# Mixing a convolution's spectra in two halves of the sequences, the second inside attention's first slots

## The chip, the cores and the metric

One core of a Trainium2 chip (trn2). The metric is the device time of one launch in microseconds, the median of several executions. The program is written by hand, engine by engine: each engine has one list of instructions, and semaphores are all that orders one engine against another.

## What is computed

16 sequences of 256 tokens with 256 channels pass through three stages: a spectral convolution, causal attention, and a mixture of 8 experts of which each token uses 2. Only the first two stages matter here.

```
x_ft = rfft(groupnorm(x))[..., :16]                 # 16 modes of each of 16 channels, 16 times, 16 sequences
out  = einsum('btix,iox->btox', x_ft * w_temb, w)   # "mixing": input channels i to output channels o
x    = x + irfft(out / norm)
t    = tokens(x)
t    = t + softmax(q k^T / 16, causal) v W_o        # q, k, v from layernorm(t)
t    = t + sum over top 2 of 8 experts of c_e * gelu(n W_fc[e]) W_proj[e],  n = layernorm(t)
```

## The kernel before

**Convolution.** TensorE makes the spectra z of all sequences (`spectra`), VectorE multiplies them with the time weights into `zr` and `zi`, both with sequence and time as columns (16 x 16 = 256). Mixing is then 4 output groups `og`, each a sum over 4 input groups of a product with `mix_r` and one with `mix_i`: 32 products of 256 columns, one PSUM bank for each `og` (`psS`, `psP`, `psO`, `psI`, L1829 to L1838). Each product is an f32 matmul, which the profile shows as two loads of weights and two passes. For each `og`, VectorE scales the bank by the inverse norm and spreads it into `spec`, 4 instructions of 32 partitions x 256 columns (L1132 to L1141). The semaphore `mix_mm` counts finished banks, `spec_ready` the 16 spreading instructions.

**Between convolution and attention.** TensorE folds Wv with Wo and Wq with Wk (`fold`, L1790), sums the router's columns (L2054), and transposes the first fold (L2059); ScalarE takes the folds out of PSUM into `vo_w` and `qk_w` (L760) and the transposes into `g_t` (L763). `upper_spec(p)` (ScalarE) and `lower_spec(p)` (VectorE, L1429) split `spec` for two sequences into three parts `spec_parts`, from which `idft_of(b)` (TensorE, L1852) makes the convolution's output of sequence b. `riders` (L1971) multiplies the router into `vo_w`.

**Attention.** `run_attention` calls each engine's slot function for k = -2 to 16. In slot k, TensorE's `pe_slot` takes sequence k through `query_keys` (L1870), `values` (L1880) and `scores` (L1906 to L1908), sequence k-1 through `probs_t` (L1920) and `attend` (L1929 to L1931), sequence k+1 through `transposes` (L1862), and sequence k+2 through `idft_of`. Slots -2 and -1 only fill this pipeline, and slot 0 has no k-1. VectorE's `dve_slot` adds the convolution's output to x (`conv_out`, L1150), takes statistics and variances (L1170 to L1183); GpSimd takes the root (L636); VectorE's `shifts` (L1190) and ScalarE's `normalise` (L820) give the normalised rows `xn`, which TensorE transposes and ScalarE copies to `xn_t`. `highest(k)` (L1207, L1208) reads the scores for the softmax. `zr` and `zi` lie in areas that attention's later buffers use again.

What sets the order of the work around the change is code written out by hand in each engine's list, with waits on semaphores in it:

```python
def run_attention(eng, body):
    for k in range(-2, B + 1):
        body(k)
```

Of the kernel before, what the change touches and what calls it, by code (L numbers as in the profile page):

```python
# [10 lines left out]
ALU = mybir.AluOpType  # L11
# [8 lines left out]
DH = D // P  # L20
# [110 lines left out]
def hybrid_block(nc, x_tok_d, x_ch_d, time_in_d, conv_in_d, w_in_d, attn_in_d, w_ffn_d, c_ident_d, c_idft_d, c_fill_d,  # L131
                 c_ids_d, c_numbers_d, out_d, slots_d):
    with ExitStack() as ctx:  # L133
# [252 lines left out]
        def gn_tile(c, n):  # L386

            at = (c * CB + n // DH) * SEQ
            return xc[:, n % DH, at:at + SEQ]

        def gn_bank(c):

            return (psS, psP)[c % 2]
# [3 lines left out]
        def on(b):  # L397

            return not isinstance(b, int) or 0 <= b < B
# [113 lines left out]
        @block.sync  # L513
        def _(sp):

            sp.dma_start(time_in[:, :], time_in_d).then_inc(ld_emb, 16)
            sp.dma_start(conv_in[:, :], conv_in_d).then_inc(ld_conv, 16)
            for c in range(CHUNKS):
                n = TOK // CHUNKS
                sp.dma_start(xc[:, :, c * n:(c + 1) * n],  # L520
                             x_ch_d.rearrange("(h p) n -> p h n", p=P)[:, :, c * n:(c + 1) * n]).then_inc(ld_xc[c], 16)
            sp.dma_start(w_in[:, :, :, :], w_in_d).then_inc(ld_qkvo, 16)
            sp.dma_start(attn_in[:, :], attn_in_d).then_inc(ld_attn, 16)
            sp.dma_start(ident[:, :], c_ident_d).then_inc(ld_ident, 16)
            sp.dma_start(idft[:, :], c_idft_d).then_inc(ld_idft, 16)
            for n, at in enumerate((slice(0, NT // 4), slice(NT // 4, NT))):
                sp.dma_start(x[:, at, :], x_tok_d.rearrange("(n p) d -> p n d", p=P)[:, at, :]).then_inc(ld_x[n], 16)
            for dst, src in ((ids[:, :], c_ids_d), (fill[:, :, :], c_fill_d)):
                sp.dma_start(dst, src).then_inc(ld_route, 16)
            sp.dma_start(numbers[:, :, :], c_numbers_d).then_inc(ld_numbers, 16)  # L530
            sp.wait_ge(ld_route, 16 * 2)
            sp.dma_start(slots_d[IDLE_ROW:IDLE_ROW + GS].rearrange("(s p) r -> p s r", p=P), fill[:, :, :]).then_inc(idle_stored, 16)
            sp.dma_start(out_d[TOK:TOK + GS].rearrange("(s p) d -> p s d", p=P), fill[:, :, 0:D]).then_inc(stored_first, 16)


            sp.wait_ge(mix_mm, NG)
            sp.wait_ge(qkvo_mm, 2)
            sp.wait_ge(exp_loaded, 1)
            sp.wait_ge(spec_ready, WI)

            def store(b, landed):

                sp.wait_ge(x2_ready, b * 2 + 2)
                sp.dma_start(out_d[bass.ds(b * SEQ, SEQ)].rearrange("(s p) d -> p s d", p=P),
                             x[:, bass.ds(b * 2, 2), :]).then_inc(landed, 16)

            with sp.Fori(0, STORED_FIRST) as b:
                store(b, stored_first)
            for b in range(STORED_FIRST, EARLY + 3):
                store(b, stored_next)  # L550
            sp.wait_ge(order_ready, 1)
            weights_in(sp, 0)
            store(EARLY + 3, stored_next)
            weights_in(sp, 1)
            store(EARLY + 4, stored_next)
            sp.wait_ge(first_ready, 4)
            sp.wait_ge(scattered_early, SENT * EARLY)
            load_group(sp, 0)
            weights_in(sp, 2)
            for b in range(EARLY + 5, B - 1):  # L560
                store(b, stored_next)


            sp.wait_ge(meta_read, 2)
            sp.wait_ge(xg_t_mm, 1)
            load_group(sp, 1)
            weights_in(sp, 3)
            store(B - 1, stored_last)
            weights_in(sp, 4)

            sp.wait_ge(plan_ready, 1)
            for e in range(E):
                at_row = sp.value_load(tail[0:1, e:e + 1], min_val=e * REGION, max_val=e * REGION + TOK)
                sp.dma_start(slots_d[bass.ds(at_row, GS)].rearrange("(s p) r -> p s r", p=P),
                             fill[:, :, :]).then_inc(filled_up, 16)


            planned(sp, AHEAD)
            slots_there(sp)
            sp.wait_ge(idle_stored, 16)  # L580
            sp.wait_ge(xg_t_mm, AHEAD)
            sp.wait_ge(meta_read, 2 * AHEAD)
            load_group(sp, AHEAD)
            sp.wait_ge(xn2_ready, 2 * B)
            sp.wait_ge(pv_mm, B)
            for n in range(RESIDENT, E):
                weights_in(sp, n)
            sp.wait_ge(y_added, added_before(GROUPS))
# [134 lines left out]
        def _(act):  # L723
# [31 lines left out]
            act.wait_ge(temb_ready, 1)  # L755
            nc.scalar.activation(tpow[:, :], tabs[:, :], ACT.Exp, scale=-1.0).then_inc(exp_loaded, 1)

            for n, (w, bank) in enumerate(((vo_w, psT1), (qk_w, psG))):
                act.wait_ge(qkvo_mm, n + 1)
                nc.scalar.activation(w[:, :, 0:D], bank[:, :].rearrange("p (h d) -> p h d", h=DH), ACT.Copy).then_inc(qkvo_ready, 1)  # L760

            def copy(out, src, done, **kw):
                nc.scalar.activation(out, src, ACT.Copy, **kw).then_inc(done, 1)  # L763

# [73 lines left out]
            def act_slot(k):  # L838
# [32 lines left out]
                    normed_in(k + 1)  # L871
                if on(k - 3) and k < B:
                    normalise(k - 3, k, 0, rows[:, 2 * k - 6:2 * k - 4, :], xn2_ready)
                if k % 2 == 0 and on(k + 4):
                    upper_spec(k // 2 + 2)
                if k == EARLY + 4:
# [115 lines left out]

            act.wait_ge(vot_mm, 1)
            copy(g_t[:, :, :], psT2[:, :], vot_ready)
            act.wait_ge(spec_ready, WI)
            upper_spec(0)
            act.wait_ge(ride_mm, 1)
            nc.scalar.activation(vo_w[:, :, D:D + E], psT1[:, 0:DH * E].rearrange("p (h e) -> p h e", h=DH),  # L1000
                                 ACT.Copy).then_inc(ride_ready, 1)
# [5 lines left out]
        def _(dve):  # L1007
# [118 lines left out]
            for g in range(NG):  # L1126
                dve.wait_ge(dft_mm, g + 1)
                for z, c in ((zr, 0), (zi, 1)):
                    v.tensor_tensor(z[:, g, :, :], banks[g][:, 0:B * HT],
                                    temb[:, c:c + 1, :].broadcast_to([P, B, HT]), ALU.mult).then_inc(z_ready, 1)  # L1130

            dve.wait_ge(inv_ready, 1)  # L1132
            for o in range(WI):
                og, j = o // 4, o % 4
                if j == 0:
                    dve.wait_ge(mix_mm, og + 1)
                quarter = slice(32 * j, 32 * j + 32)
                v.tensor_tensor(spec[:, :].rearrange("p (b t o) -> p b t o", b=B, o=WI)[:, :, :, o],
                                banks[4 + og][quarter, 0:B * HT],
                                inv[quarter, og * HT:(og + 1) * HT].unsqueeze(1).broadcast_to([32, B, HT]),  # L1140
                                ALU.mult).then_inc(spec_ready, 1)  # L1141

            last = len(BATCHES) - 1

# [287 lines left out]
            def dve_slot(k):  # L1432
# [42 lines left out]
                    statistics(k + 2, 2)  # L1475
                if on(k + 2):
                    variances(k)
                if on(k - 1):
                    attn_out(k - 1)
                if k == EARLY + 4:  # L1480
# [238 lines left out]
            def dve_group(g, par):  # L1719
# [23 lines left out]
                else:  # L1743
# [6 lines left out]
                    hidden(g, 3)  # L1750
                    x_lower(g + 1)

            dve.wait_ge(colsum_mm, 1)
            v.scalar_tensor_tensor(vo_w[:, :, D + E:VW], psV[:, 0:E].unsqueeze(1).broadcast_to([P, DH, E]), -1.0 / D, router,
                                   ALU.mult, ALU.add).then_inc(route_w, 1)

            dve.wait_ge(spec_ready, WI)
            lower_spec(0)
            dve.wait_ge(ld_x[0], 16)
            run_attention(dve, dve_slot)  # L1760
            alone(x2_ready, 2 * B)
# [5 lines left out]
        def _(pe):  # L1767
# [58 lines left out]

            pe.wait_ge(gn_rs, CHUNKS)
            pe.wait_ge(inv_step, 1)
            for og in range(NG):  # L1829
                for g in range(NG):  # L1830
                    for n, (w, z) in enumerate(((mix_r, zr), (mix_i, zi))):
                        if og == 0:
                            pe.wait_ge(z_ready, 2 * g + n + 1)
                        ins = mm(banks[4 + og][:, 0:B * HT],
                                 w[:, g, og * 4:(og + 1) * 4].rearrange("p o x c -> p (o x c)"),
                                 z[:, g].rearrange("p b t -> p (b t)"), start=(g == 0 and n == 0),
                                 stop=(g == NG - 1 and n == 1))
                ins.then_inc(mix_mm, 1)  # L1838

            pe.wait_ge(ld_attn, 16)  # L1840
            pe.wait_ge(ld_ident, 16)
# [55 lines left out]
            def scores(b):  # L1897

                pe.wait_ge(gt_ready, b + 1)
                if later(b):  # L1900
                    pe.wait_ge(probs_ready, b * 2)
                for s in range(2):
                    block = psS[:, s * P:(2 * s + 1) * P]
                    q = [g_t[:, hh, s * P:(s + 1) * P] for hh in range(DH)]
# [31 lines left out]
                mm(psP[:, KNOWN_AT:KNOWN_AT + E], counting[:, 1, :], carry_known[:, :], start=True, stop=True).then_inc(known_mm, 1)  # L1936

            def pe_slot(k):
                if on(k):
                    query_keys(k)  # L1940
                    values(k)
# [7 lines left out]
                    idft_of(k + 2)  # L1949
                if k == -2:  # L1950
                    riders()
                if on(k + 1):
                    transposes(k + 1)
                if on(k - 1):
# [98 lines left out]
            for hh in range(DH):  # L2053
                ins = mm(psV[:, 0:E], counting[:, 1, :], router[:, hh, :], start=(hh == 0), stop=(hh == DH - 1))  # L2054
            ins.then_inc(colsum_mm, 1)
            pe.wait_ge(qkvo_ready, 1)
            for a in range(DH):
                for hh in range(DH):
                    ins = nc.tensor.transpose(psT2[:, a * SEQ + hh * P:a * SEQ + (hh + 1) * P],  # L2059
                                              vo_w[:, hh, a * P:(a + 1) * P], ident[:, :])  # L2060
            ins.then_inc(vot_mm, 1)
            pe.wait_ge(qkvo_ready, 2)
            pe.wait_ge(mask_ready, 2)
            run_attention(pe, pe_slot)
            run_groups(pe, pe_group)

# [56 lines left out]
```

## Time and profile before

| | |
|---|---|
| time, median of 3 runs | 664.49 us (664.35 to 665.49) |
| the profiled execution: its time | 666.99 us |
| its span, first to last instruction | 665.2 us |
| TensorE busy | 611.6 us (92%) |
| VectorE busy | 478.5 us (72%) |
| ScalarE busy | 415.5 us (62%) |
| GpSimd busy | 385.9 us (58%) |
| mean granted clock of TensorE | 0.98 of full speed |
| mixing, folds and slots -2 to 0 | about 35 to 72 us of the span |
| attention's slots from 1 on | about 72 to 200 us |
| experts | the rest |

Busy shares are means over stages with different limits, so the change has to be read from the stretch in which it lies. In that stretch TensorE is the busiest engine, but not always busy. A granted clock of 1.00 is 2.4 GHz, one of 0.50 is 1.2 GHz. The 1.8 us between span and time lie around the program's instructions. A row of the timeline stands for neighbouring instructions of one kind: its first number is the start of the first one, its second the time from there to the end of the last, and starts of TensorE's passes overlap the ends of those before.

### The profile page before, as it was taken

To read this page: it belongs to the slowest core of one execution; us is meant where nothing else is said; L and a number is where in the kernel's file an instruction comes from. 1 tells how busy PE (TensorE), PEld (TensorE's weight loads), DVE (VectorE), ACT (ScalarE), POOL (GpSimd) and SP (SyncE) were. 2 spreads that over 40 slices of the span, in tenths; PEclk is the share of its full clock that TensorE was granted. 3 is DMA by queue.
4 is the path that set the end of the run, shared out by engine and by line. 5 is a ranking of instruction groups with operands and counts; after the bars stand their busy time and mean duration, and the time that the engine had idled before them with its cause. 6 is when DMAs were issued, how large, how long until landed. Compare 5 with 4: busy or idle time off the path is not lost. (4 is left out here: it accounts for less than half of the span.)

```text
span 665.2 us, 15083 instructions
## 1 busy us (share of the span) xinstructions
PE 611.6 (92%) x4662; PEld 581.9 (87%) x4662; DVE 478.5 (72%) x1146; ACT 415.5 (62%) x732; POOL 385.9 (58%) x284
## 2 busy tenths in 40 slices
PE   2795999999968899999999999999999999999993
PEld 2684888888857899999999999999999999999993
DVE  7654468789858678877787787778778687766661
ACT  3803667776746787777665656657566665657661
POOL 5101111485747668545767677676666767687773
PEclk9997999999988899999999999999999999999998
DMA  8900000133887673782313223131231313221211
GB/s 345 306 21 0 17 32 33 66 123 96 305 268 250 210 205 83 187 295 38 66 32 58 39 33 63 32 64 33 50 47 32 64 32 56 34 34 32 34 25 16
DMA packets 37596, 62.46 MB, mean 94 GB/s; under 512 B 3696, under 2 KB 32944, under 8 KB 36400
## 3 DMA queue, kind: packets, MB, share of 16 engines
q1 hardware_dynamic: 15360, 35.11, 15.3%
q0 software_dynamic: 13296, 18.00, 15.0%
q10 hardware_dynamic: 8896, 8.82, 5.2%
q8 instruction: 21, 0.34, 0.2%
q14 instruction: 23, 0.19, 0.1%
HBM read 37.02 MB, written 24.89 MB: 93 GB/s over the span
## 5 line engine op out<-in xcount | busy, mean ns | idle before, releaser
L695 POOL TENSOR_TENSOR pj_lo<-w_ffn,pj_hi 128x1024 fp32r<-128x1024 f32 x68 | 164.4, 2423 | 88.4 <-ACT pj_hi L763 87.6
L1640 DVE TENSOR_TENSOR fc_lo<-w_ffn,fc_hi 128x1024 fp32r<-128x1024 f32 x78 | 107.9, 1416 | 60.6 <-ACT fc_hi L763 59.0
L684 POOL DMA_INDIRECT out<-y,add_id x71 | 112.2, 1580 | 46.8 <-issue 39.8
L763 ACT ACTIVATE pj_hi<-w_ffn 128x1024 fp32r x78 | 81.8, 1058 | 85.6 <-PE psO L2032 62.7
L2032 PE MATMUL psP<-pj_hi,h_hi 128*128 128x256 f32 x312 | 92.9, 298 | 8.9 <-DVE h_lo L1640 8.7
L763 ACT ACTIVATE fc_hi<-w_ffn 128x1024 fp32r x78 | 79.1, 1053 | 25.3 <-issue 24.8
L2032 PE MATMUL psP<-pj_lo,h_hi 128*128 128x256 f32 x312 | 88.5, 284 | 0.0
L2032 PE MATMUL psP<-pj_hi,h_lo 128*128 128x256 f32 x312 | 88.3, 283 | 0.0
L646 POOL DMA_INDIRECT slots<-rows,slot x64 | 68.2, 1066 | 20.7 <-issue 18.0
L636 POOL TENSOR_TENSOR roots<-ve,power 128x6 f32<-128x6 f32 (+2 forms) x20 | 23.5, 1175 | 93.7 <-DVE ve L1183 86.8
L2032 PE MATMUL psO<-pj_hi,h_hi 128*128 128x256 f32 x256 | 73.0, 285 | 0.0
L2032 PE MATMUL psO<-pj_lo,h_hi 128*128 128x256 f32 x256 | 72.8, 284 | 0.0
L2032 PE MATMUL psO<-pj_hi,h_lo 128*128 128x256 f32 x256 | 72.4, 283 | 0.0
L2032 PEld LDWEIGHTS psP<-pj_hi,h_hi 128*128 128x128 f32 x312 | 59.6, 191 | 11.5 <-issue 10.9
L2013 PE MATMUL psT<-x_lo,fc_hi 128*128 128x256 f32 (+1 forms) x312 | 62.0, 280 | 0.0
L2013 PE MATMUL psT<-x_hi,fc_hi 128*128 128x256 f32 (+1 forms) x312 | 61.7, 279 | 0.0
L2013 PE MATMUL psT<-x_hi,fc_lo 128*128 128x256 f32 (+1 forms) x312 | 61.4, 277 | 0.0
L2032 PEld LDWEIGHTS psP<-pj_hi,h_lo 128*128 128x128 f32 x312 | 59.9, 192 | 0.0
L2032 PEld LDWEIGHTS psP<-pj_lo,h_hi 128*128 128x128 f32 x312 | 59.9, 192 | 0.0
L921 ACT ACTIVATE psT<-psT 128x512 f32<-128x512 f32 (+1 forms) x78 | 42.8, 549 | 18.9 <-PE psT L2013 18.6
L1640 DVE TENSOR_TENSOR h_lo<-psT,h_hi 128x512 fp32r<-128x512 f32 (+1 forms) x78 | 49.6, 642 | 3.6 <-ACT h_hi L763 1.0
L2032 PEld LDWEIGHTS psO<-pj_hi,h_lo 128*128 128x128 f32 x256 | 49.5, 193 | 0.0
(360 smaller groups left out, 1598.3 us busy)
## 6 DMA issues: line engine op xcount, KB each, us to landing
w_ffn<-in_w_ffn SPq DMA_DIRECT2D x8, 2048.0 KB, 9.7
xg<-slots ACTq DMA_DIRECT2D x29, 265.0 KB, 3.0
xc<-in_x_ch SPq DMA_DIRECT2D x4, 1024.0 KB, 8.4
out<-x SPq DMA_DIRECT2D x16, 256.0 KB, 2.2
x<-in_x_tok SPq DMA_DIRECT2D x1, 3072.0 KB, 24.6
slots<-fill SPq DMA_DIRECT2D x9, 265.0 KB, 2.6
out<-y,add_id POOLq DMA_INDIRECT x71, 3.9
w_in<-in_w_in SPq DMA_DIRECT2D x1, 1024.0 KB, 13.5
```

The source lines that it names most:

```text
L636: nc.gpsimd.tensor_tensor(roots[:, k + 2, first:end], ve[:, first:end], power[:, first:end], ALU.pow).then_inc(roots_ready, 1)
L646: nc.gpsimd.indirect_dma_start(slots_d, bass.IndirectOffsetOnAxis(ap=slot[:, n, t:t + 1], axis=0), rows[:, t, :], None).then_inc(scattered ...
L684: nc.gpsimd.indirect_dma_start(out_d, bass.IndirectOffsetOnAxis(ap=add_id[:, s:s + 1], axis=0), y[:, s, :], None, compute_op=ALU.add).then ...
L695: nc.gpsimd.tensor_tensor(pj_lo[:, 4 * a:4 * a + 4, :], w_ffn[:, bass.ds(e, 1), (2 + a) * DFF:(3 + a) * DFF].rearrange("p a (c d) -> p (a ...
L763: nc.scalar.activation(out, src, ACT.Copy, **kw).then_inc(done, 1)
L921: nc.scalar.activation(h, h, ACT.Gelu).then_inc(gelu_done, 1)
L1640: v.tensor_tensor(out, whole, upper.bitcast(F32), ALU.subtract).then_inc(done, 1)
L2013: ins = mm(hidden_in(g, c)[:, f % 2, :], w[:, hh, f * P:(f + 1) * P], m[:, hh, 0:parts_of(g) * P], start=(n == 0), stop=(n == 5))
L2032: ins = mm(bank[:, 0:D], w[:, s * P:(s + 1) * P], m[:, f, :], start=(f == 0 and n == 0), stop=(f == FC - 1 and n == 2))
```

## The change

The 32 products of 256 columns become 64 of 128 columns. The first half (sequences 0 to 7) is mixed where all was mixed before, in the same four banks. Of the second half (sequences 8 to 15), output group 0 is mixed ahead of the transposes of the fold, groups 1 and 2 behind `riders` in slot -2, and group 3 behind `idft_of(1)` in slot -1; group 3 uses bank `psT1`. VectorE spreads them (`spec_of`) in slots -2, -1, -1 and 0. ScalarE begins `upper_spec(0)` ahead of its copies of the folds, and VectorE `lower_spec(0)` ahead of its column sums. TensorE's waits for `qkvo_ready` and `mask_ready` move from the front of attention to slot 0, and two waits are new on it: the scores of sequence 0 wait for the spreading of the second half's group 0, and slot 1 waits at its front for all 32 spreading instructions.

```diff
+        def mix_bank(half, og):
+            return (psS, psP, psO, (psI, psT1)[half])[og]
+        def of_half(half):
+            return slice(half * B // 2, (half + 1) * B // 2)
...
-            for n, (w, bank) in enumerate(((vo_w, psT1), (qk_w, psG))):
-                act.wait_ge(qkvo_mm, n + 1)
-                nc.scalar.activation(w[:, :, 0:D], bank[:, :].rearrange("p (h d) -> p h d", h=DH), ACT.Copy).then_inc(qkvo_ready, 1)
...
+            act.wait_ge(spec_ready, WI)
+            upper_spec(0)
+            for n, (w, bank) in enumerate(((vo_w, psT1), (qk_w, psG))):
+                act.wait_ge(qkvo_mm, n + 1)
+                nc.scalar.activation(w[:, :, 0:D], bank[:, :].rearrange("p (h d) -> p h d", h=DH), ACT.Copy).then_inc(qkvo_ready, 1)
             act.wait_ge(vot_mm, 1)
             copy(g_t[:, :, :], psT2[:, :], vot_ready)
-            act.wait_ge(spec_ready, WI)
-            upper_spec(0)
...
+            def spec_of(half, og):
+                n = of_half(half)
+                cols = B // 2 * HT
+                dve.wait_ge(mix_mm, half * NG + og + 1)
+                for j in range(4):
+                    quarter = slice(32 * j, 32 * j + 32)
+                    v.tensor_tensor(spec[:, :].rearrange("p (b t o) -> p b t o", b=B, o=WI)[:, n, :, 4 * og + j],
+                                    mix_bank(half, og)[quarter, 0:cols],
+                                    inv[quarter, og * HT:(og + 1) * HT].unsqueeze(1).broadcast_to([32, B // 2, HT]),
+                                    ALU.mult).then_inc(spec_ready, 1)
...
                 if on(k + 2):
                     variances(k)
+                if k == -2:
+                    spec_of(1, 0)
+                if k == -1:
+                    spec_of(1, 1)
+                    spec_of(1, 2)
+                if k == 0:
+                    spec_of(1, 3)
                 if on(k - 1):
                     attn_out(k - 1)
...
+            def mix_of(half, og):
+                if half:
+                    pe.wait_ge(spec_ready, min(4 * og + 4, 12))
+                if half and og == NG - 1:
+                    pe.wait_ge(ride_ready, 1)
...
-                        ins = mm(banks[4 + og][:, 0:B * HT],
+                        ins = mm(mix_bank(half, og)[:, 0:B // 2 * HT],
                                  w[:, g, og * 4:(og + 1) * 4].rearrange("p o x c -> p (o x c)"),
-                                 z[:, g].rearrange("p b t -> p (b t)"), start=(g == 0 and n == 0),
+                                 z[:, g, of_half(half)].rearrange("p b t -> p (b t)"), start=(g == 0 and n == 0),
...
             def pe_slot(k):
+                if k == 0:
+                    pe.wait_ge(qkvo_ready, 2)
+                    pe.wait_ge(mask_ready, 2)
+                if k == 1:
+                    pe.wait_ge(spec_ready, 2 * WI)
...
                 if k == -2:
                     riders()
+                    mix_of(1, 1)
+                    mix_of(1, 2)
+                if k == -1:
+                    mix_of(1, 3)
...
+            mix_of(1, 0)
             pe.wait_ge(qkvo_ready, 1)
```

TensorE's list from the folds to the first slot's `query_keys`. Before, in one piece (psT<-w_in and psG<-w_in are the folds, psV<-attn_in the column sums, psT<-ident,vo_w the transposes of the fold, psI<-idft_parts `idft_of`, psT<-vo_w,g_t the `riders`, psG<-ident,xn the `transposes`):

```order
L1790 MATMUL psG<-w_in 128x256 x4
L2054 MATMUL psV<-attn_in 128x8 x2
L2059 MATMUL psT<-ident,vo_w 128x128 [waits qkvo_ready]
...
L1852 MATMUL psI<-idft_parts,spec_parts 128x256 [waits spec_upper,spec_lower,mask_ready,qkvo_ready]
L1852 MATMUL psI<-idft_parts,spec_parts 128x256
L1971 MATMUL psT<-vo_w,g_t 128x8 [waits route_w,vot_ready]
...
L1852 MATMUL psI<-idft_parts,spec_parts 128x256 [waits x1_ready,spec_lower,spec_upper]
L1852 MATMUL psI<-idft_parts,spec_parts 128x256
L1862 MATMUL psG<-ident,xn 128x128 [waits xn_ready]
...
L1870 MATMUL psG<-xn_t_94,qk_w 128x256 [waits xnt_ready]
```

The same stretch of the changed kernel; of each group of 8 mixing products the first stands here:

```order
L2093 MATMUL psV<-attn_in 128x8 x2
L1859 MATMUL psS<-zr,mix_r 128x128 [waits z_ready,spec_ready]
...
L2099 MATMUL psT<-ident,vo_w 128x128 [waits qkvo_ready]
...
L1880 MATMUL psI<-idft_parts,spec_parts 128x256 [waits spec_lower,spec_upper]
...
L2010 MATMUL psT<-vo_w,g_t 128x8 [waits route_w,vot_ready]
...
L1859 MATMUL psP<-zr,mix_r 128x128 [waits spec_ready]
...
L1859 MATMUL psO<-zr,mix_r 128x128 [waits spec_ready]
...
L1880 MATMUL psI<-idft_parts,spec_parts 128x256 [waits x1_ready,spec_lower,spec_upper]
...
L1859 MATMUL psT<-zr,mix_r 128x128 [waits ride_ready,spec_ready]
...
L1890 MATMUL psG<-ident,xn 128x128 [waits xn_ready]
...
L1898 MATMUL psG<-xn_t_94,qk_w 128x256 [waits xnt_ready,mask_ready,qkvo_ready]
```

Four groups of 8 products have come between the folds and the first `query_keys`, each in a place of its own.

VectorE's list in slot 0, from `conv_out(2)` to `highest(0)` (x<-psI,x is `conv_out`, st, mv and ve are the statistics, nmax is `highest`). Before:

```order
L1150 TENSOR_TENSOR x<-psI,x 128x512 [waits idft_mm]
L1170 BN_STATS st<-x 128x6 [waits x1_ready]
...
L1183 TENSOR_SCALAR ve<-mv 128x2
L1207 TENSOR_REDUCE nmax<-psS 128x1 [waits s_mm]
L1208 TENSOR_REDUCE nmax<-psS 128x1
```

And of the changed kernel:

```order
L1164 TENSOR_TENSOR x<-psI,x 128x512 [waits idft_mm]
L1184 BN_STATS st<-x 128x6 [waits x1_ready]
...
L1197 TENSOR_SCALAR ve<-mv 128x2
L1148 TENSOR_TENSOR spec<-psT,inv 32x128 [waits mix_mm]
L1148 TENSOR_TENSOR spec<-psT,inv 32x128 x3
L1221 TENSOR_REDUCE nmax<-psS 128x1 [waits s_mm]
L1222 TENSOR_REDUCE nmax<-psS 128x1
```

The last four spreading instructions stand behind the statistics of sequence 2 and ahead of `highest(0)`.

TensorE's list at the end of slot 0 and the front of slot 1, in the changed kernel:

```order
L1936 MATMUL psS<-xn_t_94,g_t 128x128 [waits spec_ready,gt_ready]
L1937 MATMUL psS<-causal_99,ident_100 128x128
L1938 MATMUL psS<-xn_t_94,g_t 128x128
L1936 MATMUL psS<-xn_t_94,g_t 128x256
L1938 MATMUL psS<-xn_t_94,g_t 128x256
L1898 MATMUL psG<-xn_t_95,qk_w 128x256 [waits xnt_ready,spec_ready]
```

Before, the last of these rows waits for `xnt_ready` alone.

## Rows read from the trace of the kernel before

**Rows 1.** Windows: busy time by engine, then clock, DMA share, GB/s.

```profile
72.00:186.00 114.00, 112.83 (x610) 96.23 (x610) 89.60 (x400) 78.76 (x209) 51.95 (x49) 1.00 0.31 106
186.00:230.00 44.00, 33.01 (x218) 30.46 (x217) 30.86 (x85) 28.74 (x46) 29.48 (x25) 0.88 0.74 243
```

**Rows 2.** Timeline of TensorE, mixing to slot 1.

```profile
35.11 0.70 PE L1834 MATMUL psS<-zr,mix_r 128*128 128x256 f32 x2
...
49.03 1.89 PE L1790 MATMUL psT<-w_in 128*128 128x256 f32 x8
...
52.84 0.64 PE L2059 MATMUL psT<-ident,vo_w 128*128 128x128 f32 x4
56.21 0.48 PE L1852 MATMUL psI<-idft_parts,spec_parts 96*128 96x256 f32 x2 [2.73 <-DVE spec_parts L1429]
56.52 0.96 PE L1971 MATMUL psT<-vo_w,g_t 128*128 128x8 f32 x8
...
61.94 1.11 PE L1862 MATMUL psG<-ident,xn 128*128 128x128 f32 x4 [3.83 <-ACT xn L820]
63.74 3.78 PE L1870 MATMUL psG<-xn_t,qk_w 128*128 128x256 f32 x8 [0.69 <-ACT xn_t L763]
...
71.81 1.89 PE L1870 MATMUL psG<-xn_t,qk_w 128*128 128x256 f32 x8
```

**Rows 3.** Windows of the same stretch.

```profile
58.00:60.00 2.00, 0.11 (x1) 0.00 (x0) 1.55 (x7) 0.83 (x2) 0.92 (x1) 0.50 0.00 0
...
66.00:68.00 2.00, 2.00 (x6) 1.58 (x5) 0.00 (x0) 0.44 (x1) 0.00 (x0) 0.50 0.00 0
```

**Rows 4.** Timeline of VectorE, last spreading to slot 0.

```profile
49.23 2.45 DVE L1138 TENSOR_TENSOR spec<-psI,inv 32x256 f32<-32x256 f32 x4 [1.02 <-PE psI L1834]
...
56.79 0.69 DVE L1150 TENSOR_TENSOR x<-psI,x 128x512 f32<-128x512 f32 x1 [0.73 <-PE psI L1852]
...
58.97 0.68 DVE L1429 TENSOR_TENSOR spec_parts<-spec,spec_parts 32x512 fp32r<-32x512 f32 x1
60.60 0.16 DVE L1190 SCALAR_TENSOR_TENSOR shift<-mv,roots 128x2 f32<-128x2 f32 x1 [0.95 <-POOL roots L636]
...
70.04 0.69 DVE L1150 TENSOR_TENSOR x<-psI,x 128x512 f32<-128x512 f32 x1 [5.94 <-PE psI L1852]
...
72.10 0.28 DVE L1207 TENSOR_REDUCE nmax<-psS 128x1 f32<-128x128 f32 x1
```

**Rows 5.** Timeline of ScalarE.

```profile
53.52 0.60 ACT L763 ACTIVATE g_t<-psT 128x512 f32<-128x512 f32 x1 [0.24 <-PE psT L2059]
...
60.80 1.09 ACT L820 ACTIVATE xn<-x,shift,roots 128x256 f32<-128x256 f32 x2 [1.94 <-DVE shift L1190]
63.09 0.60 ACT L763 ACTIVATE xn_t<-psG 128x512 f32<-128x512 f32 x1 [1.20 <-PE psG L1862]
```

**Rows 6.** Timeline of TensorE, the experts' last groups.

```profile
628.59 0.39 PE L2013 MATMUL psV<-x_hi,fc_hi 128*128 128x128 f32 x2
...
632.38 0.39 PE L2013 MATMUL psT<-x_hi,fc_lo 128*128 128x128 f32 x2
```

**Rows 7.** Timeline of TensorE, slot 2 from `query_keys(2)` to `query_keys(3)`.

```profile
79.41 1.89 PE L1870 MATMUL psG<-xn_t,qk_w 128*128 128x256 f32 x8
...
82.97 0.49 PE L1920 MATMUL psP<-ident,p_b 128*128 128x128 f32 x3
83.22 0.48 PE L1852 MATMUL psI<-idft_parts,spec_parts 96*128 96x256 f32 x2
...
84.04 0.71 PE L1929 MATMUL psO<-v_b,p_t 128*128 128x264 f32 x2
...
85.48 0.38 PE L1906 MATMUL psS<-xn_t,g_t 128*128 128x128 f32 x2
...
85.76 0.44 PE L1908 MATMUL psS<-xn_t,g_t 128*128 128x128 f32 x2
...
87.01 1.89 PE L1870 MATMUL psG<-xn_t,qk_w 128*128 128x256 f32 x8
```

More of the change, by code:

```diff
@@ L533, in _ @@
             sp.dma_start(out_d[TOK:TOK + GS].rearrange("(s p) d -> p s d", p=P), fill[:, :, 0:D]).then_inc(stored_first, 16)
-            sp.wait_ge(mix_mm, NG)
+            sp.wait_ge(mix_mm, 2 * NG)
             sp.wait_ge(qkvo_mm, 2)
             sp.wait_ge(exp_loaded, 1)
-            sp.wait_ge(spec_ready, WI)
+            sp.wait_ge(spec_ready, 2 * WI)
             def store(b, landed):
@@ L873, in act_slot @@
                     normalise(k - 3, k, 0, rows[:, 2 * k - 6:2 * k - 4, :], xn2_ready)
+                if k == B // 2 - 4:
+                    act.wait_ge(spec_ready, 2 * WI)
                 if k % 2 == 0 and on(k + 4):
@@ L1130, in _ @@
                                     temb[:, c:c + 1, :].broadcast_to([P, B, HT]), ALU.mult).then_inc(z_ready, 1)
-            dve.wait_ge(inv_ready, 1)
[L1133 to L1141, printed above, removed]
+            def spec_of(half, og):
[8 more added lines that the diff above has]
+                                    ALU.mult).then_inc(spec_ready, 1)
+            dve.wait_ge(inv_ready, 1)
+            for og in range(NG):
+                spec_of(0, og)
             last = len(BATCHES) - 1
@@ L1751, in dve_group @@
                     x_lower(g + 1)
+            dve.wait_ge(spec_ready, WI)
+            lower_spec(0)
             dve.wait_ge(colsum_mm, 1)
@@ L1755, in _ @@
                                    ALU.mult, ALU.add).then_inc(route_w, 1)
-            dve.wait_ge(spec_ready, WI)
-            lower_spec(0)
             dve.wait_ge(ld_x[0], 16)
@@ L1828, in _ @@
             pe.wait_ge(inv_step, 1)
-            for og in range(NG):
+            def mix_of(half, og):
[3 more added lines that the diff above has]
+                    pe.wait_ge(ride_ready, 1)
                 for g in range(NG):
@@ L1833, in _ @@
                             pe.wait_ge(z_ready, 2 * g + n + 1)
-                        ins = mm(banks[4 + og][:, 0:B * HT],
+                        ins = mm(mix_bank(half, og)[:, 0:B // 2 * HT],
                                  w[:, g, og * 4:(og + 1) * 4].rearrange("p o x c -> p (o x c)"),
-                                 z[:, g].rearrange("p b t -> p (b t)"), start=(g == 0 and n == 0),
+                                 z[:, g, of_half(half)].rearrange("p b t -> p (b t)"), start=(g == 0 and n == 0),
                                  stop=(g == NG - 1 and n == 1))
                 ins.then_inc(mix_mm, 1)
+            for og in range(NG):
+                mix_of(0, og)
             pe.wait_ge(ld_attn, 16)
@@ L1901, in scores @@
                     pe.wait_ge(probs_ready, b * 2)
+                else:
+                    pe.wait_ge(spec_ready, WI + 4)
                 for s in range(2):
@@ L2061, in _ @@
             ins.then_inc(vot_mm, 1)
-            pe.wait_ge(qkvo_ready, 2)
-            pe.wait_ge(mask_ready, 2)
             run_attention(pe, pe_slot)
```

## The prediction

> **What bounds the kernel now.** I read the windows first, to see where TensorE is the limit. In slots 1 to 14 it is: 112.83 of 114 us busy, at full clock [rows 1]. One slot there takes 7.60 us, from `query_keys(1)` at 71.81 to `query_keys(2)` at 79.41 and on to 87.01 [rows 2, 7]. So whatever moves the 71.81 moves all slots behind it by as much. The stretch between attention and the experts (186 to 230 us) waits for transfers that the slots themselves issue, so it should move along whole. The question is thus one of a single date: when does `query_keys(1)` start?
>
> The timeline of TensorE says what 35.11 to 71.81 is made of [rows 2]. Mixing runs without a gap from 35.11 to 49.03, 13.9 us: 64 passes of 256 columns at 0.217 us. Then TensorE waits 2.73 us for the first `spec_parts`, 3.83 us for `xn`, and 0.69 us for `xn_t`. In these waits its clock falls: it is 0.50 of full speed, 1.2 GHz, in 58 to 60 us, after those nearly idle stretches, and still 0.50 at 66 to 68 us, with the engine fully busy [rows 3]. `query_keys(0)` therefore takes 3.78 us where slot 1's takes 1.89. The reader is to see two losses: idle time of some 7.3 us, and work done at half the clock. Behind the idle time stands a serial chain from the last spreading (ends 51.68, [rows 4]) through ScalarE, VectorE and GpSimd to `xn`.
>
> **The price of a pass of 128 columns.** 128 passes of 128 columns take the place of 64 of 256. The trace has no such pass in mixing. The nearest rows are those of the experts' half groups, where every pass of 128 columns has its own load of weights: 34 passes in 632.38 - 628.59 = 3.79 us, 0.1115 us each [rows 6]. These are of the faster f32 format, which matters for the streaming, not for the load. The other row is from the scores, in the same f32 as mixing: two passes of 128 columns and a small third between 85.48 and 85.76, so at most 0.14 us each [rows 7]. The lower end is half of 0.217, 0.108 us. I take 0.112, because half of the 256-column pass and the experts' rows agree on it; 0.14 stays for the range. Halving then costs only 0.4 us in all, and a group of 8 products takes 1.8 us, a half 7.2 us.
>
> The Trainium skill, "TensorE: Matmul & The Clock Gate", section "LDWEIGHTS (loading the stationary operand)", has a load take its column count over 1.2 GHz, 107 ns for 128 columns whatever is streamed behind it. That speaks against the change, for the number of loads doubles with the number of products. By that rule, if a load did not hide behind the stream, a pass would be 107 ns of load and 107 ns of stream, and nothing would be halved. That loads hide in this kernel is what the 0.1115 us of the half groups shows.
>
> **The price of a spreading instruction.** Four of 256 columns take 2.45 us, 0.61 each [rows 4]. The lower bound for 128 columns is half, 0.31; the upper is 0.61, if width did not count. The shortest VectorE instruction shown takes 0.16 us for 2 columns [rows 4], so I take 0.16 plus half of the remaining 0.45, 0.385 us, or 1.54 for a bank.
>
> **The new dates on TensorE**, each from the one before it:
> - First half from 35.11, 7.2 us: 42.3. VectorE's last bank follows, 1.6 us later with the hand-over, at 43.9, against 51.68 before. Even if the chain behind it (upper, lower, first `idft_of`) took the 4.5 us that it took before (51.68 to 56.21, [rows 2, 4]), it would be there at 48.4, when TensorE comes to it (below). So this wait of 2.73 us is gone.
> - Folds and column sums, 52.84 - 49.03 = 3.8 [rows 2]: 46.1. Group 0 of the second half, 1.8: 47.9. Transposes to ScalarE's start, 53.52 - 52.84 = 0.68, and its copy of 0.60 [rows 2, 5]: 49.2, with `idft_of(0)` inside that time, at about 48.4. ScalarE reaches its copies of the folds late, behind the two copies of `upper_spec(0)`, at about 45.3 if each takes the 0.60 us of its other copies, but `qkvo_ready` is asked for only at 47.9: no cost.
> - `riders` 1.0: 50.2. Groups 1 and 2, 3.6: 53.8. `idft_of(1)`, 56.52 - 56.21 = 0.3 [rows 2]: 54.1. Group 3, 1.8: 55.9.
> - Is `xn` there by then? `idft_of(0)` at 48.4, VectorE 0.58 later, 58.97 - 56.79 = 2.2 for its statistics [rows 2, 4]: 51.2. Queued there now are one bank (1.54) and `lower_spec(1)` (0.68), longer than the 1.63 us that the root took beside them before (58.97 to 60.60), then the shift, 0.16: 53.6. ScalarE, 1.09 [rows 5]: 54.7. It is ready 1.2 us before TensorE asks, so the wait of 3.83 us is gone too, and the path is TensorE's own work.
> - `transposes(0)`, at full clock 0.68 until ScalarE starts, copy and hand-over 0.65 [rows 5]: `query_keys(0)` at 57.2, against 63.74.
>
> **Slot 0.** At full clock it is slot 2's 7.60 us without `probs_t` (83.22 - 82.97 = 0.25) and `attend` (85.48 - 84.04 = 1.44), so 5.91 us [rows 7]: TensorE could begin slot 1 at 63.1. But there it must now wait for all 32 spreading instructions, and the last four are queued on VectorE behind `conv_out(2)` and its statistics. `idft_of(2)` comes 83.22 - 79.41 - 0.25 = 3.56 after `query_keys(0)` [rows 7], at 60.8; VectorE starts 0.6 later, needs 72.10 - 70.04 = 2.06 for addition and statistics [rows 4], and then 1.54: 65.0. So a new wait of 2.0 us stands where there was none, and `query_keys(1)` starts at about 65.2. Behind that wait are queued `query_keys(1)` and all of slot 1; ScalarE and VectorE wait for those. `highest(0)` is late by the same four instructions, but its reader, the softmax, has until `probs_t(0)`, 3.56 us after `query_keys(1)`. The two banks spread in slot -1, 3.1 us, delay `shifts` of sequence 1: `conv_out(1)` at 54.7, its statistics until 56.8, the banks until 59.9. ScalarE is busy with `g_t` until 59.7 (57.2 + 1.9 + 0.6), and `xn` is there at 59.9 + 0.16 + 1.09 = 61.1, when TensorE wants it: this costs nothing, with no margin.
>
> **The sum.** 71.81 - 65.2 = 6.6 us gained. Seen as a balance: idle time of 7.3 us goes, the work at half clock (2.6 us: `query_keys(0)` 1.9, the rest in `transposes(0)` and `values(0)`) goes, together 9.9; what comes is 0.4 for the halving, 0.5 at `riders`, 0.7 at `xn_t` and 2.0 at slot 1, leaving 6.3, near the 6.6 of the dates. The profiled execution took 666.99 us (span 665.2), so that of the changed kernel should take 660.4. The median of the runs is 2.5 us below the profiled execution; from it I forecast 664.49 - 6.6 = 657.9 us.
>
> **Rivals.**
> - *The passes are dearer.* At 0.14 us, 128 of them cost 3.6 us more, and the gain is 3.0: 661.5. The scores' row speaks for it, the experts' rows against it. Chance 0.12.
> - *Slower: loads do not hide behind streams of 128 columns.* All of mixing lies on TensorE's path before and after, so the gain is gone when a pass takes 0.112 + 6.6/128 = 0.163 us, and if it took the 0.217 us of a 256-column pass, the kernel would be 6.8 us slower, 671.3. Against it stand both rows with 128 columns. Chance 0.05. The page's rule on loads gives this case when nothing overlaps.
> - *The clock falls all the same.* In the new filling, TensorE has half a microsecond of waiting and a microsecond of `riders`, whose passes stream 8 columns. If it ran 10 us at 1.2 GHz as it does now, that would cost 4 to 5 us: gain 2, 662.5. Against it: the clock fell only after two waits of 2.73 and 3.83 us with 1.9 us of work between. Chance 0.09.
> - *The handover moves differently.* In 186 to 230 us the clock is 0.88 on average [rows 1], so some 10 us are at half speed, in several spells after waits. One spell more or less, with 3 us of busy work in it, is 1.5 us either way. That widens the likeliest case.
> - *Nothing comes through*: a wait in slots 1 to 4 for something that keeps its date. I find none in the lists. Chance 0.04.
> - *The wait at slot 1 is small.* If VectorE is faster than I make it (0.31 us each), it falls to 1.7 us, and a spell at the handover drops out: gain 8.5, 656. Chance 0.08.
> - *My forecast*, gain 5 to 8: 0.62.
>
> **How the numbers follow.** A measurement tells 0.2%, 1.3 us, from no change. Faster takes all but the slower case and the one in which nothing comes through, less a little of the dear passes: 0.90; same 0.04; slower 0.06. The range takes in the handover's spell and the 0.31 us below (655.5), and the price of 0.14 us above (662.0).
>
> **What would show it.** In the changed profile: mixing's passes 0.11 us apart, the first half done at 42.3; clock 1.00 from 35 to 72; no wait of TensorE for `xn` in slot -1; `query_keys(0)` 1.9 us long at about 57.2; a wait of about 2 us for VectorE's `spec` ahead of `query_keys(1)` at about 65.2; slots of 7.60 us behind it. A clock of 0.50 anywhere in 42 to 66, or passes over 0.13 us apart, makes the prediction wrong.

## The result, and the profile after

| | before | after |
|---|---|---|
| time, median | 664.76 us (664.35 to 665.49, 4 runs) | 658.81 us (656.83 to 660.52, 4 runs) |
| the profiled execution: time, span | 666.99, 665.2 us | 656.83, 655.0 us |
| TensorE busy | 611.6 us | 607.1 us |
| VectorE busy | 478.5 us | 482.5 us |
| mean granted clock of TensorE | 0.980 | 0.991 |

The ratio is 0.9902, with a 95% interval from 0.9876 to 0.9927: 0.98% faster, 6.5 us of 664.76; the difference of the medians is 5.95. The forecast was 657.9 us, a gain of 6.6.

TensorE's timeline from mixing to slot 1 answers to [rows 2]. L1859 is mixing, L1810 a fold, L2099 the transposes of the fold, L1880 `idft_of`, L2010 `riders`, L1890 `transposes`, L1898 `query_keys`:

```profile
35.34 0.49 PE L1859 MATMUL psS<-zr,mix_r 128*128 128x128 f32 x2
...
42.59 1.89 PE L1810 MATMUL psT<-w_in 128*128 128x256 f32 x8
...
46.41 0.47 PE L1859 MATMUL psS<-zr,mix_r 128*128 128x128 f32 x2
...
48.27 0.60 PE L2099 MATMUL psT<-ident,vo_w 128*128 128x128 f32 x4
48.63 0.49 PE L1880 MATMUL psI<-idft_parts,spec_parts 96*128 96x256 f32 x2
49.56 1.06 PE L2010 MATMUL psT<-vo_w,g_t 128*128 128x8 f32 x8 [0.44 <-ACT g_t L767]
50.47 0.47 PE L1859 MATMUL psP<-zr,mix_r 128*128 128x128 f32 x2
...
54.37 0.39 PE L1859 MATMUL psT<-zr,mix_r 128*128 128x128 f32 x2
...
56.16 0.60 PE L1890 MATMUL psG<-ident,xn 128*128 128x128 f32 x4
57.54 1.97 PE L1898 MATMUL psG<-xn_t,qk_w 128*128 128x256 f32 x8 [0.78 <-ACT xn_t L767]
...
65.28 2.00 PE L1898 MATMUL psG<-xn_t,qk_w 128*128 128x256 f32 x8 [1.73 <-DVE spec L1148]
```

The reader is to see four things in these rows. The first half's 64 passes take 42.59 - 35.34 = 7.25 us, 0.113 each. The two long waits of before are not there. `query_keys(0)` takes 1.97 us instead of 3.78. And `query_keys(1)` has a wait of 1.73 us that it did not have, for VectorE's `spec`; it starts at 65.28, against 71.81.

The windows of the changed kernel answer to [rows 3]. The clock (third number from the right) stays at 1.00, 2.4 GHz, where it was 0.50:

```profile
58.00:60.00 2.00, 2.00 (x10) 1.74 (x10) 1.81 (x6) 0.46 (x1) 0.00 (x0) 1.00 0.00 0
60.00:62.00 2.00, 2.00 (x14) 1.77 (x13) 0.39 (x1) 1.79 (x5) 0.00 (x0) 1.00 0.01 4
```

VectorE's timeline answers to [rows 4]. It shows the four banks of the second half (`psS`, `psP`, `psO`, `psT`), of which the last stands between the statistics of sequence 2 and `highest(0)`:

```profile
51.27 1.56 DVE L1148 TENSOR_TENSOR spec<-psS,inv 32x128 f32<-32x128 f32 x4
...
56.63 1.55 DVE L1148 TENSOR_TENSOR spec<-psP,inv 32x128 f32<-32x128 f32 x4
58.21 1.56 DVE L1148 TENSOR_TENSOR spec<-psO,inv 32x128 f32<-32x128 f32 x4
59.81 0.16 DVE L1204 SCALAR_TENSOR_TENSOR shift<-mv,roots 128x2 f32<-128x2 f32 x1
61.61 0.69 DVE L1164 TENSOR_TENSOR x<-psI,x 128x512 f32<-128x512 f32 x1 [1.65 <-PE psI L1880]
...
63.68 1.54 DVE L1148 TENSOR_TENSOR spec<-psT,inv 32x128 f32<-32x128 f32 x4
```

The engine was idle for 1.65 us just ahead of `conv_out(2)`, and then made TensorE wait 1.73 us for instructions that it could have done in that time: the last mixing product stands ahead of `transposes(0)` at 56.16.

**A common origin.** The first mixing product starts at another time in each profile, from 34.73 to 35.94 us. So the runs below are compared by the time from that product to `query_keys(1)`: 71.81 - 35.11 = 36.70 us before, 65.28 - 35.34 = 29.94 after. The change gains 6.76 us there. In idle time and clock this is made up as follows. TensorE's waits were 2.73 + 3.83 + 0.69 = 7.25 us and are 0.44 + 0.78 + 1.73 = 2.95, which is 4.30 less; keeping the clock up is worth 2.65 (the experiment "Only the clock"); halving costs about 0.47. That makes 6.48, and 0.15 more is a short wait ahead of `idft_of(1)` that is gone too.

Part of the 6.76 is lost again later. Up to `query_keys(15)`, at 180.22 us before and 174.12 after, it is 145.11 and 138.78 us from the first mixing product, a gain of 6.33: slot 1 takes 7.70 us instead of 7.60, and slot 11 8.24 instead of 7.91.

### The profile page after: what moved, and what is told of

Read it like the earlier page. It is cut to its first block and busy times, and to the rows that moved or that the text cites. A ratio compares the mean times of both kernels' runs of the same rounds, so it can differ in the third digit from the quotient of the medians.

```text
span 655.0 us, 15232 instructions
## 1 busy us (share of the span) xinstructions
PE 607.1 (93%) x4726; PEld 579.8 (89%) x4726; DVE 482.5 (74%) x1162; ACT 415.7 (63%) x732; POOL 385.9 (59%) x284
## 3 DMA queue, kind: packets, MB, share of 16 engines
q1 hardware_dynamic: 15360, 35.11, 15.5%
## 5 line engine op out<-in xcount | busy, mean ns | idle before, releaser
L1661 DVE TENSOR_TENSOR fc_lo<-w_ffn,fc_hi 128x1024 fp32r<-128x1024 f32 x78 | 109.9, 1440 | 57.1 <-ACT fc_hi L767 55.8
```

The source lines that it names most:

```text
L1661: v.tensor_tensor(out, whole, upper.bitcast(F32), ALU.subtract).then_inc(done, 1)
```

## The experiments

Medians are over all timed executions of a run, each against the kernel before on the same chip.

| run | to `query_keys(1)` | median | before | ratio, 95% interval |
|---|---|---|---|---|
| changed kernel, second time | 29.93 us | 659.62 us | 664.95 us | 0.9912 (0.9890 to 0.9934) |
| last bank early | 28.04 | 657.10 | 664.95 | 0.9895 (0.9870 to 0.9920) |
| halves in a row | 34.72 | 662.84 | 664.95 | 0.9966 (0.9950 to 0.9981) |
| kernel before, clock kept up | 34.05 | 663.34 | 664.95 | 0.9972 (0.9959 to 0.9984) |
| changed kernel, third time | 29.93 | 659.15 | 664.49 | 0.9913 (0.9886 to 0.9941) |
| handover filled | 29.93 | 657.91 | 664.49 | 0.9892 (0.9865 to 0.9919) |
| reordered | 27.15 | 656.67 | 664.49 | 0.9874 (0.9847 to 0.9902) |
| reordered and filled | 27.14 | 654.74 | 664.49 | 0.9859 (0.9827 to 0.9891) |

### The changed kernel again

The first profile was 10.2 us shorter in span than the one before, more than the 6.5 us that TensorE's timeline accounts for.

> The changed kernel unaltered. Up to query_keys(1) nothing should differ from its first profile: that product starts at 65.3 us, against 71.8 before the change, 6.5 us of gain. Its first profiled span was 10.2 us shorter than that of the kernel before. Theory H (the further 3.7 us are luck of the clock between attention and experts, 180 to 230 us): the runs scatter over some 3 us, the profile shows another number of spells at half clock there, and the median gain is 5.5 to 7.5 us. Rival (the change speeds up the experts too): the span is again 655 us and the median gain is about 10 us.

The span is 658.0 us here, the runs lie from 656.54 to 660.23 us, and the way to `query_keys(1)` is the same to 0.01 us. A third time, beside the later runs:

> The changed kernel unaltered, on the same chip as the three others, for the comparison: query_keys(1) 29.9 us after the first mixing product, runs between 656.5 and 660.5 us.

Median 659.15 us, span 656.7. The gains by the ratios, 6.5, 5.9 and 5.8 us, are not above the 6.76 on the way to `query_keys(1)`, so nothing beyond it shows in the medians. The further 3.7 us of the first comparison belong to two single executions: the profiled one of the kernel before took 666.99 us, 2.2 above its median, and that of the changed kernel 656.83, 2.0 below its own. From `query_keys(1)` to the end of the span the three profiles take 589.7, 592.2 and 591.3 us, the one before 593.4. Up to `query_keys(15)` the three agree to 0.02 us; what scatters lies behind it. In the 44 us of the handover that answer to 186 to 230 us of [rows 1], the clock was 0.96, 0.92 and 0.92, against 0.88. The first line is of the first profile, the second of the second:

```profile
179.47:223.47 44.00, 34.35 (x249) 31.73 (x248) 31.43 (x89) 30.54 (x49) 32.69 (x27) 0.96 0.75 249
```

```profile
179.99:223.99 44.00, 33.76 (x238) 31.01 (x237) 30.98 (x85) 29.28 (x47) 29.75 (x25) 0.92 0.76 242
```

How much of it is chance and how much comes with the shift is not settled by four profiles.

### Only the clock

The kernel before, with products that nobody reads in its two long waits:

```diff
                     riders()
+                if k == -1:
+                    idle_products(16, psS)
                 if on(k + 1):
                     transposes(k + 1)
...
+            def idle_products(count, bank):
+
+                for n in range(count):
+                    mm(bank[:, 0:P], mix_r[:, n % NG, 0:4].rearrange("p o x c -> p (o x c)"), ident[:, :],
+                       start=True, stop=True)
...
             ins.then_inc(vot_mm, 1)
+            pe.wait_ge(spec_ready, WI)
+            idle_products(10, psP)
```

> The kernel before, with 10 products of 128 columns in TensorE's wait for the first spec_parts and 16 in its wait for xn; nobody reads what they write. Nothing is moved, only the clock should stay at 2.4 GHz. Theory (2.6 us of the 9.9 that the change takes away is work at half clock): query_keys(0) at 63.3 (the transposes before it are faster) and 1.9 us long, query_keys(1) at 69.2 to 69.4, gain 2.4 to 2.6 us. Rival (the clock does not depend on these waits): still 71.8, or later by what the products delay.

The clock stayed at 1.00 from 52 to 72 us, and TensorE's timeline reads:

```profile
53.99 2.40 PE L1970 MATMUL psP<-ident,mix_r 128*128 128x128 f32 x20
56.88 0.48 PE L1852 MATMUL psI<-idft_parts,spec_parts 96*128 96x256 f32 x2 [0.49 <-DVE spec_parts L1429]
...
58.61 3.74 PE L1970 MATMUL psS<-ident,mix_r 128*128 128x128 f32 x32
62.61 0.66 PE L1862 MATMUL psG<-ident,xn 128*128 128x128 f32 x4 [0.27 <-ACT xn L820]
63.95 1.99 PE L1870 MATMUL psG<-xn_t,qk_w 128*128 128x256 f32 x8 [0.69 <-ACT xn_t L763]
...
69.83 1.89 PE L1870 MATMUL psG<-xn_t,qk_w 128*128 128x256 f32 x8
```

From the first mixing product (35.78) to `query_keys(1)` it is 34.05 us, 2.65 less than before. That is the share of the clock in the change's 6.76 us. It also shows that the clock fell because TensorE was idle in these waits: nothing else was altered. The whole kernel gained 0.28%, 1.9 us (1.1 to 2.7 by its interval), which agrees with the 2.65.

### The two halves in a row

The same passes of 128 columns, the same early start of `upper_spec(0)`, but no product between other work:

```diff
-            return (psS, psP, psO, (psI, psT1)[half])[og]
+            return (psS, psP, psO, psI)[og]
...
-            for og in range(NG):
-                mix_of(0, og)
+            for half in range(2):
+                for og in range(NG):
+                    mix_of(half, og)
...
                     riders()
-                    mix_of(1, 1)
-                    mix_of(1, 2)
-                if k == -1:
-                    mix_of(1, 3)
...
-            mix_of(1, 0)
```

with all eight `spec_of` in a row on VectorE too.

> Both halves in passes of 128 columns, but one straight after the other, ahead of the folds; all else as in the changed kernel. Theory (the gain is from the second half's products standing in waits): mixing ends at 49.6 instead of 49.0, idft_of(0) follows the folds at about 54, xn is ready near 60, TensorE idles some 4 to 5 us before it; query_keys(1) at 68 if the clock stays up, at 70 to 71 if it falls; gain 1 to 4 us over the kernel before. Rival (the gain is from spectra that are there earlier for the chain behind them, filling does not matter): nearly the full 6.5 us, since the first half's spreading ends at 44 here too. Rival (the clock alone matters): the gain is 2.6 us or nothing, by whether the clock falls.

```profile
50.17 1.89 PE L1804 MATMUL psT<-w_in 128*128 128x256 f32 x8
...
54.38 0.49 PE L1873 MATMUL psI<-idft_parts,spec_parts 96*128 96x256 f32 x2
55.31 1.06 PE L1999 MATMUL psT<-vo_w,g_t 128*128 128x8 f32 x8 [0.44 <-ACT g_t L767]
...
59.84 1.11 PE L1883 MATMUL psG<-ident,xn 128*128 128x128 f32 x4 [3.14 <-ACT xn L824]
61.74 3.75 PE L1891 MATMUL psG<-xn_t,qk_w 128*128 128x256 f32 x8 [0.78 <-ACT xn_t L767]
...
70.50 1.89 PE L1891 MATMUL psG<-xn_t,qk_w 128*128 128x256 f32 x8
```

Both halves take 50.17 - 35.78 = 14.39 us, 0.47 more than mixing did before: the price of halving. The chain through `spec_parts` starts earlier, so the wait for it is gone, but the one for `xn` stays at 3.14 us, the clock falls to 0.50 from 58 to 67 us, and `query_keys(0)` again takes 3.75 us. 34.72 us to `query_keys(1)` is a gain of 1.98.

The remaining 4.78 us of the change come from the place of the second half's products. TensorE's waits are 0.44 + 3.14 + 0.78 = 4.36 us here and 2.95 in the changed kernel, 1.4 less. The rest is the clock: from `transposes(0)` to `query_keys(1)` it is 70.50 - 59.84 = 10.66 us here, and 65.28 - 56.16 - 1.73 = 7.39 there without its new wait, 3.3 less. The fall costs more in this run than in the kernel before, where the same stretch took 71.81 - 61.94 = 9.87 us.

The rival, that early spectra are enough wherever the products stand, fell: the first half's spectra are as early as in the changed kernel. What the run can't separate is how the products' place helps. In the changed kernel they stand behind the start of the chain and inside its waits at once: `idft_of(0)` comes 13.29 us after the first mixing product, here 18.60, before 21.10. Here TensorE has all 64 products and VectorE all eight banks ahead of it.

### The last bank early

```diff
                 if on(k - 3) or on(k + 1):
                     shifts(k - 1)
+                if k == 0:
+                    spec_of(1, 3)
...
-                if k == 0:
-                    spec_of(1, 3)
                 if on(k - 1):
                     attn_out(k - 1)
```

> The changed kernel with the last bank of the second half spread ahead of conv_out(2) in slot 0, where VectorE idled for 1.65 us, and not behind its statistics. Theory (TensorE's wait of 1.73 us at slot 1 comes from the place of these four instructions): the wait goes, query_keys(1) starts at 63.5 to 63.7, and the kernel is 1.6 to 1.8 us faster than the changed one, within the scatter of the handover. Rival (the wait only moves, to the softmax or to probs_t in slot 1): query_keys(1) starts early, but query_keys(2) still at 72.9.

```profile
57.90 1.97 PE L1898 MATMUL psG<-xn_t,qk_w 128*128 128x256 f32 x8 [0.78 <-ACT xn_t L767]
...
63.74 1.89 PE L1898 MATMUL psG<-xn_t,qk_w 128*128 128x256 f32 x8
...
71.34 1.89 PE L1898 MATMUL psG<-xn_t,qk_w 128*128 128x256 f32 x8
```

The wait at slot 1 is gone, `query_keys(1)` starts 28.04 us after the first mixing product, 1.89 sooner than in the changed kernel, and slot 1 takes 7.60 us. So the wait was of the place of four instructions on VectorE alone, and did not move elsewhere. The median is 2.5 us below that of the changed kernel on the same chip (659.62), but the two intervals overlap: of the runs, four of six lie from 655.55 to 657.53, two at 659.8 and 659.9. It is the trace that shows the gain.

### The order of slots -1 and 0

```diff
                 if k == -1:
-                    mix_of(1, 3)
+                    mix_of(1, 3, range(0, 2))
                 if on(k + 1):
                     transposes(k + 1)
+                if k == -1:
+                    mix_of(1, 3, range(2, NG))
...
                 if on(k - 3) or on(k + 1):
                     shifts(k - 1)
+                if k == 0:
+                    spec_of(1, 2)
+                    spec_of(1, 3)
...
                 if k == -1:
                     spec_of(1, 1)
-                    spec_of(1, 2)
-                if k == 0:
-                    spec_of(1, 3)
```

> The changed kernel with two orders altered: TensorE does half of the second half's group 3 ahead of transposes(0) and half behind them, under ScalarE's copy of xn_t (a wait of 0.78 us now); VectorE spreads only one bank in slot -1, and the other two in slot 0 between shifts and conv_out(2). Theory (both waits are of the order alone): no wait of 1.7 us at slot 1 and none of 0.8 us at query_keys(0), which starts at 56.9; query_keys(1) 5.9 us later, at 62.8, 2.5 us ahead of the changed kernel; 2.5 us faster. Rival (two banks between shifts and conv_out(2) make conv_out(2) late): xn of sequence 1 in time, but conv_out(2) 0.5 us late and nothing gained over the version with one bank moved, query_keys(1) at 63.5.

TensorE and then VectorE:

```profile
55.86 0.60 PE L1891 MATMUL psG<-ident,xn 128*128 128x128 f32 x4
56.30 0.39 PE L1859 MATMUL psT<-zr,mix_r 128*128 128x128 f32 x2
...
57.24 1.97 PE L1899 MATMUL psG<-xn_t,qk_w 128*128 128x256 f32 x8
...
63.09 1.89 PE L1899 MATMUL psG<-xn_t,qk_w 128*128 128x256 f32 x8
...
70.73 1.89 PE L1899 MATMUL psG<-xn_t,qk_w 128*128 128x256 f32 x8
```

```profile
59.01 1.58 DVE L1148 TENSOR_TENSOR spec<-psO,inv 32x128 f32<-32x128 f32 x4
60.62 1.57 DVE L1148 TENSOR_TENSOR spec<-psT,inv 32x128 f32<-32x128 f32 x4
62.23 0.69 DVE L1164 TENSOR_TENSOR x<-psI,x 128x512 f32<-128x512 f32 x1
```

Both waits are gone. From the first mixing product (35.94) to `query_keys(1)` it is 27.15 us, 2.78 less than in the changed kernel, and 0.89 less than with one bank moved. The rival was half right: `conv_out(2)` is late, at 62.23 instead of about 61.3 (0.6 us behind `idft_of(2)` at 60.67), yet slot 1 takes 7.64 us against 7.60, so this cost 0.04 us at most. 656.67 us is 2.5 us below the changed kernel beside it, with intervals that overlap a little.

### The handover

In slot 15 TensorE waits for the rows of the experts' first group (`psI<-ident,xg` in the profile), 3.88 us in the third profile of the changed kernel. Here it has 16 products that nobody reads in that place:

```diff
                 if k == B - 1:
+                    pe.wait_ge(x1_ready, B)
+                    for n in range(16):
+                        mm(psI[:, 0:P], qk_w[:, n % DH, 0:P], ident[:, :], start=True, stop=True)
                     x_transposes(0)
```

> The changed kernel with 16 products of 128 columns in TensorE's wait of 3.6 us for the first group's rows (slot 15), which nobody reads. Up to slot 15 nothing differs. Theory (the clock falls behind this wait, 0.50 to 0.68 in the 4 us after it, and how many such spells there are between 180 and 230 us scatters the runs): the clock stays 1.00 in 180 to 192, the median is 1 to 2 us below the changed kernel's, and the runs lie within 2 us. Rival (VectorE and ScalarE bound the handover, where TensorE is busy 2.2 to 3.6 of 4 us at full clock too): the spell goes, but later waits grow by as much, and the time is the same.

Windows of the changed kernel (third time), and of the filled one:

```profile
180.00:184.00 4.00, 0.55 (x3) 0.14 (x1) 3.43 (x6) 1.39 (x2) 3.39 (x3) 0.92 0.43 126
184.00:188.00 4.00, 3.57 (x15) 3.06 (x15) 0.69 (x1) 0.60 (x1) 2.40 (x3) 0.50 0.92 265
188.00:192.00 4.00, 4.00 (x27) 3.91 (x25) 2.43 (x14) 2.75 (x7) 0.49 (x1) 0.72 0.92 357
```

```profile
180.00:184.00 4.00, 4.00 (x35) 3.90 (x34) 3.43 (x6) 1.64 (x3) 3.33 (x3) 1.00 0.46 136
184.00:188.00 4.00, 3.99 (x30) 3.29 (x28) 2.08 (x9) 1.33 (x5) 2.66 (x3) 1.00 0.88 276
188.00:192.00 4.00, 2.99 (x21) 2.56 (x20) 1.96 (x10) 3.97 (x9) 2.47 (x3) 1.00 0.95 353
...
196.00:200.00 4.00, 1.43 (x7) 1.22 (x8) 1.74 (x5) 2.59 (x4) 0.72 (x1) 0.83 0.95 343
200.00:204.00 4.00, 3.58 (x22) 3.37 (x21) 3.50 (x6) 3.75 (x7) 3.48 (x2) 0.74 0.64 248
```

The spell of 0.50 behind the wait is gone, but another appears 12 us later, at the next group's rows. TensorE did not wait for these in the changed kernel (first line, third time) and waits 2.16 us in the filled one (second line):

```profile
197.42 0.60 PE L2030 MATMUL psS<-ident,xg 128*128 128x128 f32 x4
```

```profile
197.80 0.66 PE L2033 MATMUL psS<-ident,xg 128*128 128x128 f32 x4 [2.16 <-DMA xg<-slots]
```

Counted from the first mixing product (35.48 and 35.73), these products start at 161.94 and 162.07 us: what the filling saved is used up here by waiting for a transfer. The profiles thus speak for the rival. The median is 1.2 us lower (657.91 against 659.15), which the two intervals do not tell apart; that the scatter would shrink to 2 us did not come, the runs lie from 656.95 to 659.31. With the reordering as well:

> Both of the last two changes together. If both are what they are taken for and independent: query_keys(1) at 62.8, clock 1.00 in the handover, 3.5 to 4.5 us below the changed kernel, about 655 us. If the handover absorbs what is saved there: as with the reordering alone, about 657 us.

654.74 us is 9.75 us below the kernel before and 4.4 below the changed one beside it; the clock was 1.00 in all 44 us of the handover. It has the lowest median of this study, though its interval overlaps that of the reordering alone (656.67 us). One of its six runs took 659.09 us.

## Why the prediction was right

**The single date.** Predicted 65.2 for `query_keys(1)`, measured 65.28. The gain there was 6.6 by the sum and is 6.53 by the profile's dates, 6.76 from the first mixing product on. The time went the way of that date: 6.5 us by the ratio, 5.9 and 5.8 in the two later comparisons, with 6.33 left at `query_keys(15)`. That all slots behind would take 7.60 us was not quite so. In the kernel before, slots 6, 10 and 14 take 8.0 to 8.2 us as well and move along; slots 1 and 11 of the changed kernel lose 0.1 and 0.3 us that the sum did not have.

**Price of a pass.** 0.112 us chosen, 0.113 measured; 0.4 us for halving predicted, 0.47 measured. The experts' half groups were the right row to read, and the upper end of 0.14 was not. The rivals in which passes are dearer, or loads do not hide at all, are out. The Trainium skill's rule on loads ("TensorE: Matmul & The Clock Gate", "LDWEIGHTS (loading the stationary operand)"), the column count over 1.2 GHz, gives an estimate of 107 ns for 128 columns. This trace agrees with it as a lower bound for mixing, whose passes each have such a load and are 0.113 us apart.

**Price of a spreading instruction.** 0.385 chosen, 0.39 measured (1.54 to 1.57 for a bank). A fixed part of 0.16 us and half of the rest was the right reading.

**The waits that go.** Both went, and the chain to `xn` was not on the path: it was ready at 54.9 (ScalarE's `xn` starts at 53.78 and takes 1.09), 1.3 us ahead of TensorE; 1.2 was predicted. The balance of the prediction, with 7.3 us of waits and 2.6 of clock going and 3.2 of new waits coming, is the one measured: 7.25, 2.65 and 2.95.

**The wait that comes.** 2.0 predicted, 1.73 measured. TensorE's own work in front of it ended at 63.55 (65.28 - 1.73) and not at 63.1, the last bank at 65.22 and not at 65.0. Most of both comes from the first mixing product, which was 0.23 us late to begin with. The rival of a small wait, 1.7 us, has the same number, but not by its reason: an instruction took 0.39 us, not 0.31, and no time was gained by it.

**The clock.** 2.6 us of work at half clock were put down to it. Keeping the clock up without the change gave 2.65.

**Chances.** The rival of a clock that falls in the new filling did not happen: waits of 0.44, 0.78 and 1.73 us with work between them left it at 1.00. For the profiled execution the forecast was 660.4 us, and it took 656.83. That miss of 3.6 us lies in the stretch behind attention's slots, of which the prediction had said 1.5 us either way: from `query_keys(15)` to the end of the span it takes 484.98 us before and 480.88, 483.33 and 482.44 in the three profiles after. The medians show little of it: 658.81 measured, 657.9 forecast. That the ratio's gain of 6.5 us so nearly meets the 6.6 of the sum is in part luck, since the later comparisons gave 5.9 and 5.8.

## What to carry to other kernels

When an engine that bounds everything behind it waits for a serial chain, look for a part of an earlier stage that the chain's first users do not need, and put it into the waits. Of 6.8 us here, about 4.3 were idle time and 2.65 the clock that no longer fell, less 0.5 for the smaller pieces; with the same pieces ahead of the chain only 2.0 were gained. Read the price of a halved operation from any row of that shape elsewhere in the trace, fixed cost and all. Then look for the order of the follow-up work on the helping engine: four instructions placed behind an addition they had nothing to do with cost 1.7 us, and moving them, another bank and half a bank's products won 2.8 us.

## What was not expected of the hardware

- The first mixing product started between 34.73 and 35.94 us in ten profiles whose work on TensorE is the same up to there. The work behind shifts with it, so 1.2 us of scatter is there before the change's stretch begins.
- Filling one idle stretch of 3.9 us at the handover kept the clock at 1.00 there. It fell to 0.83 and 0.74 some 12 us later, at a wait of 2.16 us that the same kernel without the filling did not have; there it had been 1.00.
- In slot 11 the changed kernel takes 8.24 us where the one before took 7.91 (most slots take 7.60), with TensorE waiting 0.50 us for `xn` instead of 0.18. The two halves in a row have it too (8.26), the kernel before with its clock kept up has not (7.92), so it comes with something that the halved kernels share. What that is stays open; it takes 0.3 us of the gain.
